# Expert rings of three, variance tiles of 99 columns and column tiles of 64 in a vision tower's kernel

## The reference

```python
h = _L0_tok_ref(x, L0_tok_ln1_w, L0_tok_W, L0_tok_ln2_w)
h = concatenate([cls_tok, h], axis=1)
h = h + _L0_attn_ref(_layernorm(h), qw, kw, vw, ow)
h = h + _L0_ffn_ref(_layernorm(h), gate_w, Wg, Wu, Wd, Sg, Su, Sd)
h = h + _L1_attn_ref(_layernorm(h), ...)   # 6 layers: attention, norm, gelu feed-forward, norm
h = h + _L1_ffn_ref(_layernorm(h), w_gate, w_up, w_down)   # FP4 blocks of 16

# the experts inside _L0_ffn_ref: each takes the C = 74 tokens that score highest for it
topk_weight, topk_idx = jax.lax.top_k(scores, C)
xg = flat_x[topk_idx]
g = einsum('ecd,eid->eci', xg, Wg)          # 16 experts, 256 -> 1024
u = einsum('ecd,eid->eci', xg, Wu)
eo = einsum('eci,edi->ecd', gelu(g) * u, Wd) * topk_weight[..., None]
flat_out = zeros.at[topk_idx].add(eo)
```

## Time and profile before

| | us |
|---|---|
| median of 3 runs (lowest to highest) | 788.56 (788.21 to 789.22) |
| time of the profiled execution | 787.6 |
| its span, first to last instruction | 785.8 |
| busy in that span: PE | 757.9 |
| PE weight loads | 701.5 |
| DVE | 555.1 |
| ACT | 426.7 |
| POOL | 247.6 |

### The profile page before, as it was taken

One profiled execution on the slowest core, in us unless ns is written; L12 is line 12 of the kernel. 1 busy time (PEld: TensorE's weight loads), 2 busy tenths in 40 slices (PEclk: granted clock), 3 DMA queues, 4 the chain that ended last, 5 costly groups with the idle time before them and its releaser, 6 DMA issues.

```text
span 785.8 us, 19872 instructions
## 1 busy us (share of the span) xinstructions
PE 757.9 (96%) x7780; PEld 701.5 (89%) x7780; DVE 555.1 (71%) x1209; ACT 426.7 (54%) x816; POOL 247.6 (32%) x299
## 2 busy tenths in 40 slices
PE   9999999899899899999999999999999999999988
PEld 8898779898898898999899999989899999989758
DVE  6787593344453377787879787787879787776796
ACT  3387422222122265757776786877678677735421
POOL 0002130211111003643462465256346614633020
PEclk9999999899999999999999999999999999999999
DMA  6001745989999220101200310111031003200001
GB/s 199 1 11 45 316 144 185 387 316 378 375 381 380 84 111 2 41 15 54 75 20 13 107 40 13 42 65 40 13 107 40 0 13 107 110 2 1 1 1 32
DMA packets 16726, 83.82 MB, mean 107 GB/s; under 512 B 2848, under 2 KB 8496, under 8 KB 10672
## 3 DMA queue, kind: packets, MB, share of 16 engines
q1 hardware_dynamic: 16688, 83.30, 29.0%
HBM read 80.50 MB, written 2.79 MB: 106 GB/s over the span
## 4 chain that ended last, share of the span: by engine, by line
PE 38%; issue 25%; POOL 19%; DVE 8%; DMA 8%; ACT 3%; POOLq 0%; SPq 0%; DVEq 0%; ACTq 0%
DMA arena<-ew_in 8%; POOL W_L L2058 7%; PE bank L1179 6%; POOL HF_L L2116 4%; POOL arena L2034 3%; PE bank L741 3%; PE bank L1212 3%; POOL WQKV_L L2058 3%; PE bank L765 2%; PE bank L891 2%; PE bank L1068 2%; PE bank L924 2%; PE bank L807 1%; POOL SQ L2077 1%; PE bank L1160 1%
## 5 line engine op out<-in xcount | busy, mean ns | idle before, releaser
L2034 POOL TENSOR_TENSOR arena<-arena,srec 111x456 f32<-111x456 f32 x56 | 52.3, 961 | 122.7 <-DVE srec L2211 122.7
L1179 PE MATMUL bank<-XGS,arena 128*64 128x74 f32 x2048 | 74.5, 231 | 9.6 <-DMA arena<-ew_in 7.1
L1179 PEld LDWEIGHTS bank<-XGS,arena 128*64 128x64 f32 x2048 | 70.5, 139 | 13.7 <-issue 13.4
L2058 POOL TENSOR_TENSOR W_L<-LW,W_H 128x256 fp32r<-128x256 f32 x96 | 68.5, 749 | 36.9 <-DVE XHL L2622 33.5
L2116 POOL TENSOR_TENSOR HF_L<-arena,HF_H 128x296 fp32r<-128x296 f32 x48 | 43.9, 937 | 76.8 <-ACT HF_H L1949 76.8
L807 PE MATMUL bank<-XHL,W_H 128*128 128x296 f32 x288 | 65.1, 307 | 0.0
L1949 ACT ACTIVATE arena<-bank,vec 128x296 f32<-128x296 f32 x96 | 48.8, 509 | 20.4 <-PE bank L807 15.5
L1376 PE MATMUL bank<-HF_L,W_H 128*128 128x296 f32 x192 | 57.4, 299 | 0.0
L1376 PE MATMUL bank<-HF_H,W_H 128*128 128x296 f32 x192 | 57.4, 299 | 0.0
L1376 PE MATMUL bank<-HF_H,W_L 128*128 128x296 f32 x192 | 57.3, 299 | 0.0
L891 PE MATMUL bank<-arena 114*128 114x111 f32 x448 | 55.1, 276 | 0.7 <-issue 0.6
(11 more groups left out here) (282 smaller groups left out, 2052.3 us busy)
## 6 DMA issues: line engine op xcount, KB each, us to landing
arena<-ew_in SPq DMA_DIRECT2D x16, 2048.0 KB, 10.3
arena<-ew_in SPq DMA_DIRECT2D x16, 1024.0 KB, 7.1
LW<-lw_in SPq DMA_DIRECT2D x12, 1024.0 KB, 4.9
LW<-lw_in SPq DMA_DIRECT2D x6, 768.0 KB, 4.4
fp_weights<-arena SPq DMA_DIRECT2D x1, 2048.0 KB, 6.4
arena<-fp_weights SPq DMA_DIRECT2D x1, 2048.0 KB, 7.3
arena<-patches_in SPq DMA_DIRECT2D x2, 864.0 KB, 7.8
LW<-lw_in SPq DMA_DIRECT2D x6, 256.0 KB, 2.6
```

The source lines that it names most:

```text
L1179: last = mm(o[lo:lo + COL_TILE, m * CAP:(m + 1) * CAP], w[:, kc, at:at + COL_TILE], XGS[:, s, kc, :], start=(kc == 0), stop=(kc == C - 1))
L2034: nc.gpsimd.tensor_tensor(v, v, srec[0:QROWS, s:s + 2, :].unsqueeze(3).to_broadcast([QROWS, 2, C * JH, KEYS]), ALU.mult).then_inc(p_ready, 1)
L2058: last = nc.gpsimd.tensor_tensor(low[:, cols], value[:, cols], high[:, cols], ALU.subtract)
```

## The change

Experts: a ring of three. The third gate-and-up buffer `GU_THIRD` takes the place of the norm buffers from `R` on, the third down buffer is the `w2` part of `LW`, so expert 2 is loaded before the loop and `w2` of layer 0 after the last down products. Loops of PE, ACT and SP have bodies of three experts (four turns), DVE's of six (two turns); steps 13 and 14 are written out behind PE's loop. Norms: three variance tiles of ceil(nt / 3), 99 or 96 tokens, so the transposes of `ln_bcast_of` have 99 rows. Encoder: value products in two column tiles of 64, and the second variance of a phase in column tiles of 64 and 35.

```diff
+ERING = 3
...
+        GU_THIRD = nc.alloc_sbuf_tensor_at("GU_THIRD", [P, EGU_N], F32, offset=R_BASE)
+        XGS_BASE = R_BASE + 4 * EGU_N
+        XGS = nc.alloc_sbuf_tensor_at("XGS", [P, ERING, C, CAP], F32, offset=XGS_BASE)
...
+        down_third = LW[:, WQKV_N + WO_N + W1_N:LW_N]
+        GU = [EW[0][:, 0:EGU_N], EW[1][:, 0:EGU_N], GU_THIRD[:, :]]
+        DOWN = [EW[0][:, EGU_N:EW_N], EW[1][:, EGU_N:EW_N], down_third]
...
         def var_tiles(nt):
 
-            return (0, P), (P, P), (nt - P, nt - 2 * P)
+            w = third(nt)
+            return 0, w, nt - w
+
+        def third(nt):
+
+            return -(-nt // 3)
...
+            sp.wait_ge(u_ready, 2)
+            load_gate_up(2, 2)
             sp.wait_ge(pos_cast, 1)
             sp.dma_start(pos_store, pos16[0:E, 0:N]).then_inc(route_stored, 16)
             sp.wait_ge(route_stored, 16)
-            load_route(0, 0)
-            load_route(1, 1)
+            for e in range(ERING):
+                load_route(e, e)
 
             sp.wait_ge(moe_pe, MOE_PE["shared"])
+            load_down(2, 2)
             load_layer(0)
             load_rest(0, "wo", LW_AT["wo"], WO_N, ld_wo)
             load_rest(0, "w1", LW_AT["w1"], W1_N, ld_w1)
+
+            def load_ahead(k, n):
+
+                sp.wait_ge(u_psum, k * 2)
+                load_gate_up(k + 2, (n + 2) % ERING)
+                if not isinstance(k, int):
+                    sp.wait_ge(shot_ready, k - 1)
+                    load_route(k + 1, (n + 1) % ERING)
+                sp.wait_ge(d_psum, k)
+                load_down(k + 2, (n + 2) % ERING)
+
+            load_ahead(1, 1)
+            with sp.Fori(0, 4) as i:
+                for n in range(2, 5):
+                    load_ahead(i * 3 + n, n)
+            sp.wait_ge(shot_ready, E - 3)
+            load_route(E - 1, (E - 1) % ERING)
+            sp.wait_ge(d_psum, E - 1)
             load_rest(0, "w2", LW_AT["w2"], W2_N, ld_w2)
-
-            def load_expert(e, s, route=True):
-
-                sp.wait_ge(u_psum, e * 2 - 2)
-                load_gate_up(e, s)
...
-                sp.wait_ge(d_psum, e - 1)
-                load_down(e, s)
...
-            def ln_var_of(seq, h, ones):
+            def ln_var_of(seq, h, ones, width=P):
...
+                w = third(nt)
+                for t, t0 in enumerate(var_tiles(nt)):
                     for c in range(nch):
                         at = VAR_AT + t * VAR_W
-                        last = mm(ln_bank(seq, h)[:, at:at + VAR_W], sq[:, h, c, t0:t0 + P], ones[:, 0:VAR_W],
-                                  start=(c == 0), stop=(c == nch - 1))
+                        for lo in range(0, w, width):
+                            hi = min(lo + width, w)
+                            last = mm(ln_bank(seq, h)[lo:hi, at:at + VAR_W], sq[:, h, c, t0 + lo:t0 + hi],
+                                      ones[:, 0:VAR_W], start=(c == 0), stop=(c == nch - 1))
...
+                    last = nc.tensor.transpose(ln_bank(seq, h)[:, t0:t0 + w], ln_rs[0:w, h, t:t + 1].to_broadcast([w, P]),
+                                               ident[0:w, 0:w])
...
-                        last = mm(o[:, i * QROWS:(i + 1) * QROWS],
-                                  Ve[0:KROWS, at_half(plan, h) * HB + b % HB, c * P:(c + 1) * P],
-                                  PTr[0:KROWS, b % PSLOTS, c, :], start=True, stop=True)
+                        width = P if plan.first else COL_TILE
+                        for lo in range(0, P, width):
+                            last = mm(o[lo:lo + width, i * QROWS:(i + 1) * QROWS],
+                                      Ve[0:KROWS, at_half(plan, h) * HB + b % HB, c * P + lo:c * P + lo + width],
+                                      PTr[0:KROWS, b % PSLOTS, c, :], start=True, stop=True)
...
-            expert_step(0, 0, 1, 1, None)
-            with pe.Fori(1, E // 2) as i:
-                expert_step((i, -1, -1), 1, (i, 0, 0), 0, (i, -1, -2))
-                expert_step((i, 0, 0), 0, (i, 0, 1), 1, (i, -1, -1))
-            expert_down(E - 1, 1)
-            expert_scatter(E - 2)
-            turn_output(E - 1)
+            expert_step(0, 0)
+            with pe.Fori(0, 4) as i:
+                for n in range(1, ERING + 1):
+                    expert_step(i, n)
+            for n in range(E - 3, E - 1):
+                expert_step(0, n)
+            expert_down((0, E - 1))
+            expert_scatter((0, E - 2))
+            turn_output((0, E - 1))
...
-                    ln_var_of((ly, 1), hy, ones_d)
+                    ln_var_of((ly, 1), hy, ones_d, COL_TILE if x else P)
...
-                    for e in range(2):
+                    for e in range(ERING):
                         f(XGS[:, e, :, :], XG[:, :, e, :], ACT.Copy).then_inc(xg_staged, 1)
...
+            with act.Fori(0, 4) as i:
+                for n in range(1, ERING + 1):
+                    expert_of(i * ERING + n, n)
...
+            with dve.Fori(0, 2) as i:
+                for n in range(6):
+                    after_turn(i, n)
+            for n in range(E - 4, E - 2):
+                after_turn(0, n)
```

More of the change, by code:

```diff
@@ L934, in patch_stats @@
                         constant_products(bank[4], 3)
-                    for t, (t0, _) in enumerate(var_tiles(NP_HALF)):
-                        last = mm(bank[5][:, at + t * VAR_W:at + (t + 1) * VAR_W], R[:, h, k, t0:t0 + P], ones_p[:, 0:VAR_W],
+                    w = third(NP_HALF)
+                    for t, t0 in enumerate(var_tiles(NP_HALF)):
+                        last = mm(bank[5][0:w, at + t * VAR_W:at + (t + 1) * VAR_W], R[:, h, k, t0:t0 + w], ones_p[:, 0:VAR_W],
                                   start=True, stop=True)
@@ L1583, in ln_root @@
                 act.wait_ge(ln_var, ln_count(seq, h))
-                f(ln_sd[:, h, :], LNB[h][:, VAR_AT:VAR_AT + 3 * VAR_W:VAR_W], ACT.Sqrt, bias=eps1[:, :]).then_inc(ln_std, 1)
+                w = third(ln_geometry(seq)[1])
+                f(ln_sd[0:w, h, :], LNB[h][0:w, VAR_AT:VAR_AT + 3 * VAR_W:VAR_W], ACT.Sqrt, bias=eps1[0:w, :]).then_inc(ln_std, 1)
             def exponent(r, p):
@@ L1613, in enc_root @@
                 act.wait_ge(ln_var, ln_count(LN_ENC, h))
-                f(ln_sd[:, h, :], ln_bank(LN_ENC, h)[:, VAR_AT:VAR_AT + 3 * VAR_W:VAR_W], ACT.Sqrt, bias=eps_sq[:, :], scale=1.0 + EPS
+                w = third(NHALF)
+                f(ln_sd[0:w, h, :], ln_bank(LN_ENC, h)[0:w, VAR_AT:VAR_AT + 3 * VAR_W:VAR_W], ACT.Sqrt, bias=eps_sq[0:w, :], scale=1.0 + EPS
                   ).then_inc(ln_std, 1)
@@ L1640, in square_mean @@
                 act.wait_ge(patch_stats_ready, h + 1)
-                f(mean_sq[:, h, :], bank[5][:, MU_AT:MU_AT + 3 * VAR_W:VAR_W], ACT.Square).then_inc(mean_squared, 1)
+                w = third(NP_HALF)
+                f(mean_sq[0:w, h, :], bank[5][0:w, MU_AT:MU_AT + 3 * VAR_W:VAR_W], ACT.Square).then_inc(mean_squared, 1)
             def token_root(h):
@@ L1647, in token_root @@
                 act.wait_ge(ln_var, ln_count(LN_TOK, h))
+                w = third(NP_HALF)
                 for t in range(3):
-                    last = f(ln_sd[:, h, t:t + 1], LNB[h][:, VAR_AT + t * VAR_W:VAR_AT + t * VAR_W + 1], ACT.Sqrt,
-                             bias=eps_var[:, h, t:t + 1])
+                    last = f(ln_sd[0:w, h, t:t + 1], LNB[h][0:w, VAR_AT + t * VAR_W:VAR_AT + t * VAR_W + 1], ACT.Sqrt,
+                             bias=eps_var[0:w, h, t:t + 1])
                 last.then_inc(ln_std, 1)
@@ L2159, in ln_recip @@
                 dve.wait_ge(ln_std, ln_count(seq, h))
-                v.reciprocal(ln_rs[:, h, :], ln_sd[:, h, :]).then_inc(ln_rstd, 1)
+                w = third(ln_geometry(seq)[1])
+                v.reciprocal(ln_rs[0:w, h, :], ln_sd[0:w, h, :]).then_inc(ln_rstd, 1)
             def ln_scale(seq, h, out):
@@ L2578, in _, with after_turn @@
             expert_hidden(2)
-            with dve.Fori(0, E // 2 - 1) as i:
-                for s in range(2):
-                    split_output(i * 2 + s)
-                    expert_onehot(i * 2 + s, i, s)
-                    if s == 0:
-                        weight_scale(i)
-                    else:
-                        weight_round(i)
-                    expert_hidden(i * 4 + (2 * s + 4))
+            def after_turn(i, n):
+                e = i * 6 + n
+                split_output(e)
+                expert_onehot(e, i * 2 + n // ERING, n % ERING)
+                part = i * 3 + n // 2
+                if n % 2 == 0:
+                    weight_scale(part)
+                else:
+                    weight_round(part)
+                expert_hidden(e * 2 + 4)
+            with dve.Fori(0, 2) as i:
[3 more added lines that the diff above has]
+                after_turn(0, n)
             for e in (E - 2, E - 1):
                 split_output(e)
-                expert_onehot(e, E // 2 - 1, e % 2)
+                expert_onehot(e, e // ERING, e % ERING)
             dve.wait_ge(scat_done, E)
```

99 lines of the change are left out of this document (44 added, 55 removed).

## The result

The changed kernel takes 775.48 us (median of 4 runs, 773.64 to 776.02) against 788.89 for the kernel before beside it: a ratio of 0.982 (95% interval 0.980 to 0.985), 13.4 us faster. I had forecast 781.5, 7 us faster. The direction held, and the mechanism in the main; one term of the sum was far too large. The profiled execution after took 776.02, the longest of the four, with a span of 774.2.

What follows compares the result with a forecast made beforehand. PE, busy 96% of the span, was taken to bound the kernel, with the expert stage bound by its loads. Terms -6.9 + 5.7 - 1.7 - 1.7 - 1.3 - 1.2 = -7.1 gave a median of 781.5 us, range 775 to 786.5.

Steps and rivals of the forecast that it cites:

- a second hole of 2.3 us: Loop's first turn, third expert's up: PE stands 2.3 us for its instruction packet, then half clock; +5.7 us in all.
- The waits of the loop: Experts' stage from 164.55 us on: the ring of three removes PE's waits for gate and up loads, -6.9 us.
- the tiles: Norms and encoder products: 99-column variance tiles (-1.7, -1.7, -1.3) and two column tiles for values and second variance (-1.2).
- The 0.69 at 142.97: PE's 0.69 us wait at 142.97, before the first hole: goes but only lengthens that hole, so 0.
- The 99-column tiles: Norms: narrower stationary tiles shorten first variances (-1.7), other norms and patch sums (-1.7) and spreads (-1.3); bounds 0 and 7.6.
- The column tiles: Encoder values and second variance: PE saves time, but only the first value bank's 0.1 us a phase counts, -1.2 us.
- the wait of 0.5 to 0.9 in place of 0.17: Sign of being right: the second norm's spread (L774) waits 0.5 to 0.9 us for DVE instead of 0.17.
- No second hole: Rival, experts' loop: packet arrives ahead of the 2 MB load or code blocks lie otherwise; 775.8 us, chance 0.20.
- The second hole without a fall: Rival, loop's third expert: the hole comes without the clock falling, 2.3 us instead of 5.7; 778.1 us, chance 0.14.
- The code stayed resident: Against the rival that the longer loop body is reread every turn; 798.6 us, chance 0.08 including two more holes.
- the column tiles ran side by side: Against the rival that the encoder's two column tiles run one after the other; +33 us, near 816, chance 0.03.
- the tiles gave their worth: Against the rival that passes saved in encoder and front all turn into waits; 787.4 us, chance 0.08.

Runs made afterwards that it cites:

- light loads: Loads issued in the experts' stage cut to 64 KB, order and waits kept: changed kernel 767.64 us, kernel before 773.73, changed without column tiles 767.60.
- moved reciprocal: Changed kernel with 64 KB expert loads, DVE's reciprocal of the second norm put ahead of its third value bank's copies: 769.94 us, against 767.64 without the move.
- one load less: Changed kernel with one load, gate and up of expert 6, cut from 2 MB to 64 KB: 773.99 us, 0.982 of the kernel before.
- long pauses: Changed kernel with 64 KB expert loads and a PE pause ahead of the loop's third expert's up, each turn: 781.60 us, against 767.64 without pauses.

## Why the prediction missed

**The step that failed** is "a second hole of 2.3 us. [...] As the one hole of this length that the trace has was followed by the fall of the clock, I take +5.7". The place was right within three products (after 27 of up, forecast 24), and so was the cause. The size was not: 0.93 us and no fall in the profiled run, so 1.1 us. Two things were taken as fixed that vary from execution to execution. First the length: with the same experts' code and loads the second hole was 0.93, 1.56, 2.21, 1.19 and 1.69 us in five profiles. I had put the packet 5 to 7.9 us behind its 2 MB issue and taken the middle; it moved 5.0 us behind (161.78 to 166.81), at the near end. Second the fall: it followed one of the five, and cost 4.0 - 2.2 = 1.8 there, not 3.4. One event of the trace of before was no sample for either. From the gate of the loop's third expert to the next gate the five profiles take 9.00, 9.65, 11.86, 9.33 and 10.60 us, which is 1.1 to 4.0 over 7.87 where I charged 5.7 (the 10.60 has another hole of 0.65 in it). The mean clocks of the changed kernel's ten runs agree: two falls of 6.8 us, as I took them, would give 1 - 0.5 x 13.7 / 774 = 0.991, and the lowest is 0.996.

Of the 6.0 us between 781.5 and 775.48 this term makes 4.6. The waits of the loop bring 0.6 more, the tiles 0.6 less in these two profiles, and the rest is that I put the median 1.0 above the profiled execution and it lies 0.5 below.

**The waits of the expert loop** were -6.9 in the forecast. They are a little more: one expert without loads takes 15.71 / 2 = 7.855 us (light loads, before), so that 94.05 - 11 x 7.855 = 7.65 us went to the loads in the earlier trace rows, 6.8 of it as idle time of PE (94.05 - 87.23). The 0.69 at 142.97 went too and came back as a longer first hole, as forecast: that event cost 6.7 - 5.9 = 0.8 more. So the experts' stage gives -7.65 - 0.7 + 0.8 + 1.1 = -6.45 (measured -6.3), where I had -1.2.

**The tiles** were right in sum, 5.9 forecast and 6.1 measured with light loads, and wrong in their split, so that the sum is luck. The 99-column tiles bring all of it, 6.1 where I had 4.7 of 7.6 at most for variances, patch sums and spreads. In the light runs 2.65 us of it lie ahead of the experts (first gate at 131.59 and 128.94), 3.7 behind. The column tiles, forecast at -1.2, bring nothing. PE's part was right, 48 short passes in 2.50 us and 24 long in 2.83 (light loads, without column tiles), and the wait of 0.5 to 0.9 in place of 0.17 came as forecast. But DVE begins its copies 1.15 us after the first value product where it was 1.19, so 0.04 earlier and not 0.1, and from there its chain is the same. Here are its nine copies and the reciprocal, without and with column tiles, light loads:

```profile
428.64 3.30 DVE L2255 TENSOR_SCALAR OB<-bank,lvec 96x148 f32<-96x148 f32 x9 [0.22 <-PE bank L915]
431.87 0.16 DVE L2192 RECIPROCAL ln_rs<-ln_sd 99x3 f32<-99x3 f32 x1
```

```profile
428.98 3.30 DVE L2255 TENSOR_SCALAR OB<-bank,lvec 96x148 f32<-96x148 f32 x9 [0.26 <-PE bank L915]
432.20 0.16 DVE L2192 RECIPROCAL ln_rs<-ln_sd 99x3 f32<-99x3 f32 x1
```

From the first copy to the reciprocal it is 3.23 and 3.22 us. That it is DVE's work and not only its order is shown by the moved reciprocal: the wait went to the next product that needs DVE.

**The rivals.** "No second hole" (775.8) has the right number by luck: there was a second hole. "The second hole without a fall" (778.1) has what four of the five profiles show, with the hole at 0.9 to 1.7 us and not 2.3. The code stayed resident, the column tiles ran side by side (64 short passes take 2.50 + 0.96 us, 32 long ones 2.83 + 1.10), and the tiles gave their worth. The rule that a block's crossing is mostly hidden (the Trainium skill, "Runtime: NRT & Kernel Launch", Instruction fetch mechanics) agrees with the light runs, without a hole in the experts, and not with the loaded ones: 3.8 to 5.4 us of holes in each profile of the changed kernel and its variants where all loads move (2.1 in the kernel before).

**What stays open.** Why some 4 to 5 us of holes come whatever the cut and the moment of the loads is not settled: they need the loads (light runs), one goes when one load goes (one load less), and they move with the code, but their length followed no rule that I tried. Nor is it settled what decides, among pauses of 2 us, whether the clock falls. In the profiles of this study 17 pauses in the experts were of 2.0 us or more, and the clock fell behind 12; of 5 between 1.5 and 2.0 behind 2; of 23 between 0.4 and 1.3 behind none, nor behind the wait of 1.17 ahead of the last down products, which every profile has.

## What to carry to other kernels

Before a term rests on one event of one trace, ask for how many executions that event is a sample: I gave a hole and a fall of the clock the full price of the only one I had seen, and that alone was 4.6 of the 6.0 us that I missed by. Runs with the traffic taken away (small loads, same order, same waits) are quiet, here within about 1 us where the full ones spread over up to 5.7 (changed) and 8.1 (before), and weigh small edits that the full runs can't. And a saving on PE ahead of a product that waits for another engine's whole queue is worth only what comes forward of that queue's start: count from the first row of the other engine's chain.

## What the runs showed of the hardware

A code packet of 16 KB that moves among full loads lets PE go on 2.2 to 2.6 us after its start, in all 34 holes of 0.25 us or more that these profiles have in the experts (147.64 to 149.96 and 166.81 to 169.20 here). A loop body of 1,212 products and weight loads was read in its first turn and ran three more with no further packet on PE's queue. A single met wait ahead of each of 80 products left the holes within two products of their places; two such waits moved the first hole by 40 products, one instruction for each of the 80. And the granted clock can fall to 1.2 GHz behind a pause of 2 us with only small loads in the queues, for 3.4 us (189.1 to 192.5 with long pauses) or 6.8 (150.7 to 157.5 in the changed kernel), or not at all.
